# New execution order and new PSUM places for a four-layer kernel on one Trainium2 core

## The chip, the core and the metric

The kernel runs on one core of a Trainium2 chip. A core has TensorE (PE: matrix products into PSUM, eight banks), VectorE (DVE), ScalarE (ACT), GpSimd (POOL) and SyncE (SP), each with an instruction queue of its own that it executes in order, and 16 DMA engines. Engines wait for one another through semaphores. The metric is the device time of one execution in microseconds (us); times of a version are given as the median of several runs.

## What is computed

Four layers on x of 4 x 512 x 256, each `x + attention(norm(x)) + feed_forward(norm(x))`:

```
xn = layernorm(x)
L0: 16-head causal attention with alibi  + ternary-weight gated FFN (groups of 64, hidden 1024)
L1: gated recurrence: causal conv of 4, l2-normed q and k, scan mem = gamma*mem + gate*k*v, group norms
    + mixture of 16 experts, top 2, capacity 128, and a shared expert
L2: single-head attention                + gated FFN whose weights are cubic splines of control points
L3: 16-head attention with rope          + 8 experts, top 2 of a softmax, bf16, and a shared expert
    (its FFN also adds its own input xn)
```

Attention per head, as everywhere: `softmax(q k^T / sqrt(d) [+ alibi, causal]) v`, then an output projection.

## The kernel before

The kernel is written as parts. A part is a few instructions of one engine for one tile: `score` is two 64-row products of keys and queries of a group of four heads into a pair of PSUM banks (L749), from which DVE's `top` takes the maximum (L1152); `prob` is the same product with the maximum subtracted (L760), which ACT's `exp` turns into `probs` (L1670); `weigh` multiplies with the values (L770). `unit` is one of eight hidden blocks of a feed-forward layer for one batch, twelve matmuls in layer 2 (three products of high and low halves), and POOL's `low` makes the low half of its result. `tern_cast` (ACT), `tern_sum` (PE), `tern_scaled` (DVE, L1045 to L1055) and `tern_out` (POOL) make one of twelve ternary weight blocks each. `stat` (DVE), `root` (POOL, L1983) and `norm` (ACT, L1574) make the normalized rows, `turn` (PE, L710) transposes them, `turned` (ACT) and `cut_low` (DVE, L1096) split them into a high and a low half.

Keys carry the layer, the batch and tile numbers: score(0,0,0,0,3) is layer 0, batch 0, head group 0. q and k of a batch are stored to DRAM (`keep`, SP) and read back regrouped by heads (`bring`, POOL, L1965, two issues of 512 KB); the maxima take the same way (`max_keep`, `max_bring`, L1971). In layer 1 POOL's `gather` fetches each token's two expert rows from the outbox by indirect DMA, four issues for a part (L2082), after the last experts' stores. In layer 2 the spline weights are made by DVE, ACT's `spline_high` (L1875) and POOL's `spline_low` (L2090); `score2` is a row block of its attention, `top2` (DVE, L1486) and `exp2` (ACT, L1899) its softmax. In layer 3 `q_low` (DVE, L1128) is the low half of the turned q and k, and POOL's `based` (L1991) and `with_xn` (L1996) add the bias and xn to x; `mixed` (DVE, L1540) and `mix_comb` (POOL, L2100) belong to the experts.

All work around the change is ordered by hand-written numbers. `PARTS` lists the parts of each engine (1098 on PE, 844 on DVE, 857 on ACT, 429 on POOL, 165 on SP). `DUE` gives each part a turn on its engine, and `Turns` sorts by it; that order is the order of the instructions. `TAKEN` gives each part of PE its first PSUM bank: 0, 2 or 4 for those that take a pair or one of a pair, 6 or 7 for single ones. `Plan` walks PE's order, notes who held a place last, and `freed` makes the new holder wait for those that read it. All waits are counted from the order by semaphores, so a new table changes the counts that are waited for and nothing else.

## Time and profile before

| | |
|---|---|
| median of 3 runs | 1232.33 us (1230.72 to 1233.26) |
| span of the profiled execution | 1229.5 us; the page gives no time outside it |
| PE busy | 1096.5 us, 89% of the span |
| DVE / ACT / POOL busy | 864.2 / 631.2 / 503.0 us |
| mean granted TensorE clock | 0.951 of full speed |
| DMA | 116.42 MB, mean 95 GB/s |

The span runs from the first to the last instruction. An engine's busy time counts its compute instructions; the rest is idle time, and the profile names what ended it. In a row of the timeline, what stands in brackets is the idle time before the instruction and the instruction or transfer that ended it. The granted clock is TensorE's, as a share of full speed: 1.00 is 2.4 GHz, 0.5 is 1.2 GHz. A matmul that stands behind a wait in the order waits too, even if its own inputs are ready. Layers take the stretches 0 to about 360 us, to 600, to 850 and to the end, with overlaps of neighbours.

### The profile page before, as it was taken

The numbers are of one execution on the slowest core, as the hardware profiler recorded it, in microseconds if no ns is written. First come the engines' busy times: TensorE is split into PE (matmuls) and PEld (weight loads), VectorE is DVE, ScalarE is ACT, GpSimd is POOL, SyncE is SP. The second block draws the span as 40 slices with busy tenths as digits, with TensorE's granted clock in tenths as the row PEclk, the third lists the DMA queues.
The fourth block names the chain that finished last, engine by engine and source line by source line (L and its number), as shares of the span: only waits on it lengthen the run. The fifth ranks groups of instructions, "written<-read, shape, count | busy, mean of one in ns | idle before, by whom it ended". The sixth has DMA issues, their size and how long they took to land.

```text
span 1229.5 us, 17428 instructions
## 1 busy us (share of the span) xinstructions
PE 1096.5 (89%) x6541; PEld 718.4 (58%) x6556; DVE 864.2 (70%) x1612; ACT 631.2 (51%) x963; POOL 503.0 (41%) x551
## 2 busy tenths in 40 slices
PE   4579999999999998999389999998789998996998
PEld 2356686765665564675268898987234543553445
DVE  6988767678658999856667326368776779668751
ACT  4445656475568875643235224252176276455473
POOL 5655748466514544413764214053331321141131
PEclk9769999999999999999689999999699999998999
DMA  5905335443260000267350000008626316317220
GB/s 178 291 10 156 81 96 161 126 123 107 49 207 35 35 35 9 82 206 243 94 52 26 1 1 1 1 26 201 156 51 155 108 45 165 92 49 173 71 72 18
DMA packets 86115, 116.42 MB, mean 95 GB/s; under 512 B 29616, under 2 KB 43280, under 8 KB 85264
## 3 DMA queue, kind: packets, MB, share of 16 engines
q1 hardware_dynamic: 47792, 70.28, 19.1%
q0 software_dynamic: 38240, 45.03, 14.7%
q8 instruction: 52, 0.85, 0.3%
q14 instruction: 31, 0.25, 0.1%
HBM read 81.54 MB, written 40.40 MB: 99 GB/s over the span
## 4 chain that ended last, share of the span: by engine, by line
PE 64%; DVE 21%; ACT 5%; issue 4%; POOL 3%; DMA 2%; another core or an unknown queue 0%; SPq 0%; ACTq 0%; DVEq 0%; POOLq 0%
PE pair L691 22%; PE bank L691 19%; PE bank L770 7%; PE pair L760 5%; PE pair L749 5%; DVE max L1152 4%; ACT probs L1670 2%; POOL gathered L2082 1%; PE pair L710 1%; PE bank L778 1%; DVE hidden L1208 1%; DVE hidden L1206 1%; DVE tern_mask L1049 1%; PE pair L790 1%; DVE mix_h L1540 1%
## 5 line engine op out<-in xcount | busy, mean ns | idle before, releaser
L1152 DVE TENSOR_REDUCE max<-pair 128x2 f32<-128x1024 f32 (+3 forms) x256 | 252.6, 1020 | 64.1 <-PE pair L749 36.6
L1670 ACT ACTIVATE probs<-pair 128x1024 f32<-128x1024 f32 (+3 forms) x256 | 213.4, 865 | 112.9 <-PE pair L760 106.4
L749 PE MATMUL pair<-ks,qs 64*128 64x512 f32 (+3 forms) x512 | 111.7, 457 | 28.7 <-DVE max L1152 13.9
L770 PE MATMUL bank<-probs,v 128*32 128x512 f32 (+3 forms) x1024 | 119.0, 542 | 2.0 <-ACT probs L1670 1.3
L760 PE MATMUL pair<-qs,ks 64*128 64x512 f32 (+3 forms) x512 | 103.8, 437 | 13.7 <-DVE max L1152 4.9
L2003 POOL TENSOR_TENSOR h_low<-hidden,h_high 128x512 fp32r<-128x512 f32 x64 | 83.3, 1307 | 77.4 <-ACT h_high L1708 77.0
L749 PEld LDWEIGHTS pair<-ks,qs 64*128 64x128 f32 x512 | 50.8, 198 | 89.2 <-DVE max L1152 35.1
L760 PEld LDWEIGHTS pair<-qs,ks 64*128 64x128 f32 x512 | 46.5, 190 | 81.2 <-ACT probs L1670 25.9
L2100 POOL TENSOR_TENSOR h<-mix_h,h 128x512 bf16<-128x512 f32 x48 | 54.8, 1169 | 75.4 <-DMA h<-comb 49.7
L1702 ACT ACTIVATE hidden<-pair 128x512 f32<-128x512 f32 x64 | 38.0, 597 | 86.5 <-PE pair L691 72.6
L2047 POOL TENSOR_SCALAR_AFFINE_SELECT probs<-probs 128x256 f32<-128x256 f32 x128 | 51.3, 411 | 65.0 <-ACT probs L1670 63.8
L1189 DVE TENSOR_TENSOR x<-bank,x 128x512 f32<-128x512 f32 x32 | 21.9, 686 | 78.6 <-PE bank L691 78.6
L1206 DVE SCALAR_TENSOR_TENSOR hidden<-hidden,pair 128x512 f32<-128x512 f32 x64 | 43.8, 684 | 41.6 <-ACT hidden L1702 41.4
L1965 POOL DMA_DIRECT2D qs<-kept x32 | 24.2, 755 | 119.4 <-DMA kept<-q_low 52.7
L1708 ACT CAST h_high<-hidden 128x512 fp32r<-128x512 f32 x64 | 39.1, 620 | 48.7 <-DVE hidden L1208 29.7
L1971 POOL DMA_DIRECT2D qs<-kept_max x32 | 24.8, 776 | 88.2 <-DMA kept_max<-max_rows 87.3
L691 PE MATMUL pair<-x,w_in 128*128 128x512 bf16 x179 | 47.4, 400 | 5.5 <-DVE mix_h L1540 1.4
L1926 ACT ACTIVATE mix_t<-pair 128x512 f32<-128x512 f32 x48 | 28.5, 599 | 44.1 <-PE pair L691 42.5
L691 PE MATMUL bank<-wo,rowsT 128*128 128x256 f32 x192 | 48.8, 385 | 1.1 <-ACT rowsT L1691 1.1
L1540 DVE SCALAR_TENSOR_TENSOR mix_h<-mix_t,pair 128x512 f32<-128x512 f32 x48 | 32.7, 685 | 22.8 <-ACT mix_t L1926 16.4
L691 PE MATMUL pair<-cut_high,w_in 128*128 128x512 f32 x128 | 45.1, 436 | 2.9 <-POOL w_in L1977 2.2
L1574 ACT ACTIVATE xn<-x,shift,rstd 128x256 f32<-128x256 f32 x64 | 36.0, 599 | 19.9 <-POOL shift L1985 19.9
(327 smaller groups left out, 2678.5 us busy)
## 6 DMA issues: line engine op xcount, KB each, us to landing
kept<-q_high SPq DMA_DIRECT2D x64, 256.0 KB, 3.7
qs<-kept POOLq DMA_DIRECT2D x32, 512.0 KB, 4.2
ks<-kept POOLq DMA_DIRECT2D x32, 512.0 KB, 5.2
kept<-q_low SPq DMA_DIRECT2D x32, 256.0 KB, 4.1
expert_in<-in_experts_in SPq DMA_DIRECT2D x16, 352.0 KB, 4.3
expert_out<-in_experts_out SPq DMA_DIRECT2D x16, 256.0 KB, 5.5
h<-comb SPq DMA_DIRECT2D x4, 1024.0 KB, 5.4
x<-in_x SPq DMA_DIRECT2D x4, 512.0 KB, 5.1
```

The lines of the kernel that those rows point to most:

```text
L691: made = mm(out, lhsT, rhs, start=start and n == 0, stop=stop and n == len(pairs) - 1)
L749: made = mm(to[:, hh, 0:n], m.qs[k][slot][r0:r0 + STACK, p, qt * P:(qt + 1) * P], m.ks[k][slot][r0:r0 + STACK, p, 0:n], start=True, stop=k ...
L760: made = mm(to[:, hh, q0:T], m.ks[k][slot][r0:r0 + STACK, p, kt * P:(kt + 1) * P], m.qs[k][slot][r0:r0 + STACK, p, q0:T], start=True, stop ...
L770: made = mm(to[32 * j:32 * j + 32, q0:T], m.v[b % 2][:, kt, G * g + j, :], m.probs[(2 * kt + j // 2) % 4][:, j % 2, q0:T], start=kt == 0, ...
L1152: V.tensor_reduce(m.max[:, g % 2, :, p, qt], to[:, :, 0:n], AX.X, ALU.max).then_inc(*s.done("top"))
L1206: V.scalar_tensor_tensor(h[:, :], h[:, :], 1.0, to[:, 0, :], ALU.add, ALU.mult).then_inc(*dve.up())
L1540: V.scalar_tensor_tensor(h, m.mix_t[j % 2][:, :], 1.0, to[:, 1, :], ALU.add, ALU.mult).then_inc(*s.done("mixed"))
L1670: A.activation(m.probs[(2 * kt + p) % 4][:, :, q0:T], to[:, :, q0:T], ACT.Exp, scale=0.25).then_inc(*s.done("exp"))
L1708: A.copy(m.h_high[k][:, j, :], m.hidden[k][j % 2][:, :]).then_inc(*s.done("high"))
L2003: Q.tensor_tensor(m.h_low[k][:, j, :], m.hidden[k][j % 2][:, :], m.h_high[k][:, j, :].bitcast(F32), ALU.subtract).then_inc(*s.done("low"))
L2047: Q.affine_select(corner, corner, [[0, 2], [1, P]], ALU.is_ge, 0.0, base=0, channel_multiplier=-1).then_inc(*s.done("causal"))
L2100: Q.tensor_tensor(m.h16[:, j, :], m.mix_h[j % 2][:, :], m.h16[:, j, :], ALU.mult).then_inc(*s.done("mix_comb"))
```

## The change

Only numbers of `DUE` and `TAKEN` are replaced: the turns of parts on all five engines, and the PSUM places. They were chosen on the mean of several drawn sets of durations and landings. The parts, their instructions, their tiles in SBUF and the transfers stay the same, and so do all functions.

661 of PE's 1098 parts keep their position, 435 of DVE's 844, 365 of ACT's 857, 138 of POOL's 429 and 94 of SP's 165. Most others move by a few positions; by five or more move 7 parts on PE, 27 on DVE, 44 on ACT, 24 on POOL and 3 on SP. 259 parts of PE get another first bank, among them 53 of score, 55 of prob, 40 of weigh and 20 of unit.

The core of the diff: the rows of which the tables differ most, and those of the parts named above. Numbers are in the order of the keys.

```diff
 DUE = {...
-    "tern_sum": "0 2 3 4 7 9 8 10 17 15 16 26",
-    "turn": "1 52 144 207 375 432 444 469 582 598 623 646 664 711 829 952",
+    "tern_sum": "0 1 3 4 7 10 8 9 16 14 17 27",
+    "turn": "2 52 143 207 375 432 445 468 582 598 623 645 654 711 829 952",
...
-    "root": "2 20 47 63 101 171 239 258 288 291 297 309 315 320 337 348",
-    "based": "6 48 52 78 319 330 342 364",
-    "with_xn": "322 332 344 366",
+    "root": "2 19 46 66 102 171 245 258 288 292 299 305 315 324 336 345",
+    "based": "6 49 53 82 319 330 347 412",
+    "with_xn": "326 346 378 413",
...
-    "gather": "283 285 286 287 289 290 293 292",
-    "spline_low": "276 277 280 279 278 281 282 284 296 294 295 298",
+    "gather": "284 285 286 287 289 291 293 294",
+    "spline_low": "276 277 278 281 282 279 280 283 295 290 297 296",
...
 TAKEN = {...
-    "tern_sum": "040400240442",
-    "turn": "2224040202422044",
+    "tern_sum": "200400240442",
+    "turn": "2244004202042044",
...
-    "qk2": "4420",
-    "v2": "76766767",
-    "score2": "6776676766677676",
-    "probs_turn": "7676677667767776",
+    "qk2": "0200",
+    "v2": "76766776",
+    "score2": "6777677677667766",
+    "probs_turn": "7676677667766776",
```

The moves that the prediction speaks of, read out of the tables: on PE tern_sum(1) goes ahead of turn(0,0), score(0,0,0,0,3) ahead of unit(0,0,5), and unit(2,0,3) ahead of score2(0,3). The place of score2(0,3) in PSUM is then freed by exp2(0,1) and no longer by exp2(0,0). On DVE gated(2,0,0), combine(2,3), weight2(0,2) and combine(2,2) go ahead of top2(0,0), with top2(0,1) right behind it, and two maxima, top(3,0,3,1,2) and top(3,0,3,1,1), ahead of q_low(3,1,0). On ACT tern_cast(2) goes among the first norms and tern_cast(3) ahead of turned(0,0). On POOL bring(0,0,0) goes behind bring(0,0,1), tern_out(5), two low, a sum and bring(0,0,2); spline_low(2,1) ahead of gather(0,0); with_xn(1) and based(3,2) from 800 and 828 us to behind root(3,3); with_xn(2) from 843 us to ahead of mix_comb(1,8); based(3,3) and with_xn(3) behind bring(3,3,3).

## Rows read from the trace of the kernel before

**Rows 1.** The page: span, busy times by engine, the chain that ended last.
```profile
span 1229.5 us, 17428 instructions
PE 1096.5 (89%) x6541; PEld 718.4 (58%) x6556; DVE 864.2 (70%) x1612; ACT 631.2 (51%) x963; POOL 503.0 (41%) x551
...
PE 64%; DVE 21%; ACT 5%; issue 4%; POOL 3%; DMA 2%; another core or an unknown queue 0%; SPq 0%; ACTq 0%; DVEq 0%; POOLq 0%
```

**Rows 2.** Stretches: length, busy of PE, PEld, DVE, ACT, POOL, clock, DMA, GB/s.
```profile
0.00:30.00 30.00, 11.92 (x37) 7.49 (x37) 20.21 (x38) 13.69 (x23) 17.11 (x20) 1.00 0.58 181
30.00:90.00 60.00, 39.04 (x199) 27.05 (x203) 52.63 (x92) 27.05 (x46) 37.07 (x37) 0.74 0.51 155
90.00:360.00 270.00, 262.93 (x2266) 180.60 (x2265) 189.94 (x357) 161.31 (x260) 154.73 (x230) 1.00 0.42 126
360.00:570.00 210.00, 195.96 (x802) 122.41 (x801) 174.90 (x398) 137.85 (x217) 81.47 (x64) 0.98 0.25 80
570.00:630.00 60.00, 37.06 (x142) 24.62 (x140) 35.14 (x77) 17.23 (x33) 41.10 (x43) 0.80 0.55 117
660.00:840.00 180.00, 179.44 (x1036) 158.98 (x1035) 89.43 (x168) 65.61 (x119) 56.26 (x43) 1.00 0.05 13
930.00:1140.00 210.00, 187.17 (x1068) 94.31 (x1073) 157.69 (x269) 110.22 (x136) 48.99 (x53) 0.95 0.43 110
```

**Rows 3.** PE's waits: what was waited for, us in total, times, longest.
```profile
PE pair L710 <- ACT xn L1574: 20.4, 2, 18.6
PE pair L749 <- DVE max L1152: 13.9, 23, 1.3
```

**Rows 4.** DVE's timeline at 15 us: start, us, line, operation.
```profile
14.97 0.69 DVE L1045 TENSOR_SCALAR tern_scale<-pair 128x512 bf16<-128x512 f32 x1 [1.43 <-PE pair L702]
```

**Rows 5.** PE's timeline, first projection and first score.
```profile
21.13 0.80 PE L691 MATMUL pair<-cut_high,wqk_high 128*128 128x512 f32 x1 [0.53 <-DVE cut_low L1096]
...
63.65 0.50 PE L749 MATMUL pair<-ks,qs 64*128 64x512 f32 x2 [2.96 <-DVE tern_mask L1055]
```

**Rows 6.** Three more stretches, columns as in the second group.
```profile
624.10:627.00 2.90, 2.90 (x14) 2.37 (x13) 1.36 (x4) 2.32 (x4) 2.29 (x3) 1.00 0.85 73
633.00:639.00 6.00, 6.00 (x17) 4.70 (x16) 5.76 (x15) 1.03 (x2) 0.00 (x0) 0.54 0.40 36
922.00:926.00 4.00, 4.00 (x20) 1.51 (x12) 2.75 (x4) 1.70 (x3) 0.00 (x0) 0.60 0.98 229
```

**Rows 7.** L1965 from 30 to 70 us: issues, and their time to landing.
```profile
L1965 POOL DMA_DIRECT2D qs<-kept x3: 716/762/798, 41.0 to 49.4; - x3
...
DMA to landing us min/median/max: 7.7/9.7/13.1
```

**Rows 8.** L2082, 584 to 606 us: ns min/median/max, first, last start.
```profile
L2082 POOL DMA_INDIRECT gathered<-outbox,slots x16: 945/949/1179, 584.6 to 604.7; - x16
```

**Rows 9.** POOL's timeline among these gathers.
```profile
589.46 1.28 POOL L2090 TENSOR_TENSOR w_in_low<-spline_raw,w_in_high 128x512 fp32r<-128x512 f32 x1
```

**Rows 10.** ACT's timeline ahead of them.
```profile
585.41 0.62 ACT L1875 CAST w_in_high<-spline_raw 128x512 fp32r<-128x512 f32 x1 [3.36 <-DVE spline_raw L1460]
```

**Rows 11.** PE's timeline at 632 us.
```profile
632.34 1.22 PE L691 MATMUL bank<-cut_high,qk 128*128 128x512 f32 x2 [4.00 <-ACT probs L1899]
```

**Rows 12.** DVE's timeline from 630 us.
```profile
630.59 0.69 DVE L1486 TENSOR_REDUCE top<-bank 128x1 f32<-128x512 f32 x1 [4.21 <-remote]
...
631.39 1.80 DVE L1435 SCALAR_TENSOR_TENSOR x<-gathered,weights,x 128x256 f32<-128x256 f32 x2
```

**Rows 13.** L1128, whole span: ns min/median/max, first and last start.
```profile
L1128 DVE TENSOR_TENSOR q_low<-turned_raw,q_high x8: 1217/1224/3746, 834.0 to 1112.5; 128x1024 fp32r<-128x1024 f32 x8
```

**Rows 14.** POOL's timeline, with_xn(3) and the idle time before a max_bring.
```profile
915.29 2.44 POOL L1996 TENSOR_TENSOR x<-x,xn 128x1024 f32<-128x1024 f32 x1
...
1160.13 0.76 POOL L1971 DMA_DIRECT2D qs<-kept_max  x1 [4.94 <-DMA kept_max<-max_rows]
```

**Rows 15.** PE's timeline at 920 us.
```profile
920.01 0.50 PE L749 MATMUL pair<-ks,qs 64*128 64x512 f32 x2 [0.81 <-DVE max L1152]
```

More of the change, by code:

```diff
@@ L325 @@
-    "prob": "2220042002044000204242442202024020242024424204420002200424202224242420240242202040222400020224240442044042040202242024040240424022424402244220422200220204240242042022420040244044044440024404404204224004402020002422420204024024022004240442404424024442000420",
-    "weigh": "77776666666666666666666677776666666677777777777766666666666666667777666666666666777766667777666677776666777777777777777777776666",
-    "back": "77677667666677777776767676766677",
-    "rows": "402004020442",
-    "out": "76677767666776767676766776667667",
@@ L330 @@
-    "unit": "2402020420004202220202044042044220422040024204202044200424402044",
-    "down": "77767677",
-    "mean": "6777",
-    "proj": "0044022402200440",
-    "gate": "7766667776676776",
+    "vals": "2020224404004244",
+    "score": "4404002400444040204022042420022420044404024240044042004400404442402044024224200020040044024400020040204204400020204020220044424002020424022244442440440240420040022442200424040402024404020002222004042204424244042024044424000242242404444202222240204200440220",
@@ new lines @@
+    "prob": "4202242002042400424044222202024020242024024204420022200442404224242420240242202040222402020224240442040442040202224202400422404022424402244224422200220202420442002022420040044044044440024404000202442000402022002422020204040404022004240402404422044442000420",
+    "weigh": "66666666666677776666666677776666777766667777777766666666666666666666777766666666666677776666777777776666777777777777777777776666",
+    "back": "67677677766677767776676776776676",
+    "rows": "442004040244",
+    "out": "67767767766776767666776777667676",
@@ L335 @@
+    "unit": "2402020420004202220242044002244240422040424024024422040442404404",
+    "down": "77666677",
+    "mean": "7776",
+    "proj": "0444022002200440",
+    "gate": "7666666767666776",
     "gamma": "4024",
     "inflow_turn": "0202",
-    "mem_turn": "77777677",
-    "shared": "0202440220420402",
-    "count": "6666",
+    "mem_turn": "77777666",
+    "shared": "0202440240420422",
+    "count": "7766",
     "logit_turn": "7777",
     "merge": "76",
-    "expert_turn": "6676777777676666",
@@ L343 @@
[L343 to L352 removed]
+    "expert_turn": "6677777777676666",
+    "expert_in": "4204242042400204",
+    "expert_fold": "7767666667767667",
+    "expert_out": "6667766676766767",
@@ L353 @@
+    "spline": "424024202404",
+    "qk2": "0200",
+    "v2": "76766776",
+    "score2": "6777677677667766",
+    "probs_turn": "7676677767766776",
+    "comb_turn": "7766",
+    "mix": "402042020240040402024220200402424220242402004224",
 }.items()}
```

8 lines of the change are left out of this document (removed), and 262 rows, old and new, of the table DUE.

## The prediction, made before the changed kernel had run

> **What bounds the kernel now.** I read the page first. [rows 1] gives a span of 1229.5 us with PE busy in 1096.5 of them (89%), and a chain that lies 64% on PE and 21% on DVE. So 133 us of idle time on PE is all that an order can win, plus what TensorE's clock gives back. Then I cut the span into stretches [rows 2]. From 90 to 360 us PE is busy 262.9 of 270, from 660 to 840 us 179.4 of 180. No order makes those much shorter, but a badly placed part can make them longer. The idle time stands elsewhere: 18.1 us before 30; 21.0 from 30 to 90, with DVE at 52.6 of 60 and the granted clock at 0.74; 14.0 from 360 to 570; 22.9 from 570 to 630, clock 0.80; 22.8 from 930 to 1140. Last I read PE's list of waits [rows 3]: the largest single one is 18.6 us for the normalized rows of layer 2 (xn, L1574), and 13.9 us in 23 pieces are for the row maxima (L1152), 0.6 us each.
>
> The whole change is order. Since each engine executes in order, its parts do the same work; a move costs or gains only where the moved part is at the head of its engine while another engine waits for what lies behind it. I compared the two tables part by part and looked up in the trace where every part that moves stands. Most moves swap neighbours: on PE seven parts of 1098 move five places or more. I cost the five places where a move meets a wait that the trace shows, and bound the rest.
>
> **Place 1, the start.** PE now does tern_sum(1) before turn(0,0). Before, it stood behind turn(0,0), and DVE waited 1.43 us for it, until 14.97 [rows 4]. DVE's ternary block can start 1.43 us earlier, and with it cut_low(0,0), which follows the block and which the first projection at 21.13 waits for [rows 5]. Against it: turn(0,0) now takes the place in PSUM that tern_scaled(0) reads, and two ternary casts go ahead of ACT's turned(0,0). Both lie beside DVE's block, so they cost nothing unless they take longer than the 4.7 us left of it (21.13 - 14.97 - 1.43). The first projection gains 1.4 us, and DVE, busy 52.6 of the next 60 us, carries that forward. At 63.65 PE has waited 2.96 us for its chain, at score(0,0,0,0,3) [rows 5]. unit(0,0,5), which had been done ahead of that wait, now stands behind it, and its matmuls, 2.9 us for a unit's twelve [rows 6] or less, lose their cover. But DVE bounds this stretch, and nothing is added to it. I take the 1.4 as kept, between 2.4 gained (one more collision of POOL with DVE gone) and 1.5 lost (2.9 - 1.4).
>
> The other edit here: on POOL bring(0,0,0), issued at 41.0, goes behind bring(0,0,1), bring(0,0,2) (49.4) and work between, so to about 51. Such an issue took 7.7 to 13.1 us to land here, median 9.7 [rows 7]. It lands at 60.7 by the median, 64.9 by the slowest with its second half 0.8 later; its first reader runs at 63.65, after a wait for DVE. I take nothing, and keep 1.3 us lost (64.9 less 63.65) as a bound.
>
> **Place 2, the gathers before layer 2.** The 18.6 us wait is a chain through POOL: sixteen gathers, 0.95 us each, first start 584.6, last 604.7 [rows 8], and behind them root(2,0), whose result the norms and then turn(2,0) wait for. In the new table spline_low(2,1), which stood inside that row at 589.46 with 1.28 us [rows 9], comes before the first gather. It needs ACT's spline_high, which starts at 585.41 and takes 0.62 [rows 10]. So: ready at 586.03, done at 587.3, first gather 587.3 - 584.6 = 2.7 us late; and the 1.28 us inside the row go. The row ends 2.7 - 1.3 = 1.4 us late, and root(2,0) with it. This is a loss at full price, since PE does nothing else there. Bounds: 0, if spline_high comes as much earlier, and 2.7.
>
> **Place 3, the hole at 632.** PE stood 4.00 us for the probabilities (L1899) [rows 11], because DVE started the maximum of score2(0,0) at 630.59 after 4.21 us which the trace puts on nothing in the kernel ("remote") [rows 12]. Two edits meet here. PE puts unit(2,0,3) before score2(0,3); a unit's matmuls, 624.1 to 627.0, take 2.9 us [rows 6], so 2.9 of the 4.0 are filled with work that had to be done anyway. But score2(0,3) also gets another place, which the second next exponential, exp2(0,1), frees instead of exp2(0,0). And DVE puts gated(2,0,0), combine(2,3), weight2(0,2) and combine(2,2) ahead of that maximum, top2(0,1) right behind it. combine(2,3) took 1.80 us in the old order [rows 12], combine(2,2) 1.0, gated 1.4, weight2 0.65 and top2 0.85, in the same timeline: 5.7 in all. If the stall stays after the same number of DVE's instructions, score2(0,3) can start 5.7 us later than at 632.34, and 5.7 - 2.9 = 2.8 are lost. If there is no stall, it is 4.2 less: 1.4 gained. The row shows the stall once and not what makes it. I take half of it (2.1), which gives 0.7 lost, and keep both ends. Behind the hole the clock was 0.54 for 6 us [rows 6], 6 x (1 - 0.54) = 2.8 us; that it comes back is a bound for the good case alone.
>
> **Place 4, POOL beside DVE at 915.** q_low of the rope layer (L1128) takes 1.22 us by the median of eight, and 3.75 once [rows 13]: at 915, where POOL runs with_xn(3) (L1996, 2.44 us) [rows 14]. 1.22 + 2.44 = 3.66, so DVE stood still for the length of POOL's operation. PE then waits 0.81 us for one maximum [rows 15] and 0.6, the mean of such waits [rows 3], for the next, and from 922 to 926 its clock is 0.60 [rows 6], which costs 4 x 0.4 = 1.6. The change puts based(3,3) and with_xn(3) behind bring(3,3,3), into POOL's 4.94 us of idle time before 1160.13 [rows 14]. They would take 2 x 2.44 = 4.9, just what is free. DVE also takes two maxima (top(3,0,3,1,2) and its neighbour) ahead of q_low now, the ones that PE waits for. Gain: 1.4 at least, 1.4 + 1.6 = 3.0 at most; I take 2.6, for DVE is late by 2.5 us for everything behind q_low. The Trainium skill (SBUF — State Buffer, "Who interferes with whom") says that a DVE operation with both inputs in SBUF and a GpSimd operation that reads SBUF hold one shared port pair in turn, each for a whole instruction, and that a maximum (tensor_reduce) never takes part. The trace agrees with its first half (3.75 us beside 1.22); by that rule the new places beside maxima cost nothing, and DVE gets back 2.44 us, so the sum would be 0.2 us worse than with my 2.6.
>
> **Place 5, everything else.** Some 150 parts of score, prob and weigh get other PSUM places or swap, and ACT and DVE swap their partners. Where PE is 97 to 100% busy, they have no idle time to win. In 360 to 570 and 930 to 1140 there are 14.0 and 22.8 us of idle time [rows 2], in gaps under 3 us each. I take 0; a tenth of these 37 us either way is 4 us.
>
> Sum: -1.4 + 1.4 + 0.7 - 2.6 + 0 = -1.9 us on the profiled span: 1229.5 to 1227.6. The median of the runs stands 2.8 us above that span, so 1232.3 - 1.9 = 1230.4, 0.15% faster. About 0.2% (2.5 us) is what a measurement of this kernel can tell from no change.
>
> **Rivals.** (A) The good ends come together: DVE's stall is gone (-1.4 for place 3), with it the low clock behind it (-2.8), the start gives 2.4 and place 4 gives 3.0. -2.4 + 1.4 - 1.4 - 2.8 - 3.0 = -8.2, so 1224.1. For it: the clock was low right behind both holes [rows 6], and nothing in the kernel makes the stall. Against: with no stall at all there is still a wait for exp2(0,1).
>
> (B) The stall stays whole: it goes to gated(2,0,0), the instruction that now stands there, and the five parts behind it. Place 3 costs 2.8, the start gives nothing under unit(0,0,5): 0 + 1.4 + 2.8 - 2.6 = +1.6, so 1233.9. For it: in the old order the four moved parts took just the DVE time behind the stall.
>
> (C) Slower, by one mechanism: a score or prob part's new place in PSUM is still being read for its last owner when PE comes to it, in order, so that PE stands and its clock falls. The pair at 920 is the measure: 0.8 us and 1.6 by the clock, 2.4 each. Against -1.9 for the rest, one new one gives +0.5, two +2.9 (1235.2), three +5.3 (1237.6), four +7.7; it decides from two on. For it: 53 score and 55 prob places change, and 23 waits for a maximum stand already [rows 3]. Against: nearly all swaps are with the next neighbour, and PE finds work at once in 97% of 90 to 360.
>
> **How the numbers follow.** My forecast 0.36, (A) 0.22, (B) 0.20, (C) 0.22. The forecast's own range is 1227 to 1234, one bound of one term either way. The range over all cases reaches from 1221 (A with a tenth of the idle time of place 5 won) to 1240 (C with four holes). Faster by over 0.2% (below 1229.9): 0.17 of the forecast, (A), and 0.02 of (B) and (C) by place 5: 0.41. Within 0.2%: 0.17 of the forecast, 0.08 of (B), 0.02 of (C): 0.27. Slower (above 1234.8): the rest, 0.32.
>
> **What would show it.** Place 1: the first L691 near 19.7 instead of 21.13. Place 2: the first gather 2.7 us later against ACT's spline_high and turn(2,0)'s wait 1.4 us longer. Place 3: the gap before score2(0,3), 4.00 us before, between 2.6 (no stall) and 6.8 (whole stall), and which DVE instruction stands behind "remote". Place 4: L1128 with a longest time near 1.25 us, and no gap of 0.81 us behind it. Place 5: PE's busy time in 90 to 360 and 660 to 840 as before. I am wrong if new gaps over 1 us stand in the attention stretches behind DVE's maxima with a clock of 0.6, or if PE's busy time grows where it was full.

## The result and the profile after

The new order is slower: 1240.11 us by the median of four runs (1236.77 to 1241.41), against 1232.34 for the kernel before in the same comparison. The ratio is 1.0065 [1.0048, 1.0083], so 7.8 us more. The prediction said 1230.4 us. The profiled execution has a span of 1237.9 us, 8.4 above that of before. Medians here and below leave out executions over 1.5% above the fastest of their kernel, which was one execution in all.

The page, as [rows 1] for the kernel before:

```profile
span 1237.9 us, 17417 instructions
...
PE 1108.4 (90%) x6542; PEld 724.8 (59%) x6556; DVE 844.2 (68%) x1612; ACT 630.4 (51%) x964; POOL 500.4 (40%) x551
...
PE 62%; DVE 17%; ACT 8%; issue 4%; DMA 4%; POOL 3%; SPq 1%; ACTq 0%; DVEq 0%; POOLq 0%
```

PE's idle time did not grow. It was 1229.5 - 1096.5 = 133.0 us and is 1237.9 - 1108.4 = 129.5. PE's busy time grew, by 11.9 us for the same matmuls. The mean granted clock fell from 0.951 to 0.945. Over the spans, 1229.5 x 0.049 = 60 us of full speed were missing before and 1237.9 x 0.055 = 68 are missing now, about as much more as the spans differ. Nobody who looks for new waits alone finds that, and the prediction looked for waits. In PE's list of waits, the two largest of [rows 3] are shorter, and one that was 2.0 us has become 7.2:

```profile
PE pair L710 <- ACT xn L1574: 18.8, 2, 16.0
PE pair L749 <- DVE max L1152: 12.1, 22, 1.5
...
PE pair L702 <- DVE hidden L1208: 7.2, 1, 7.2
```

The last one stands in layer 0, at 55 us, and comes up again under place 1.

To find the place, I took how much later each of PE's parts starts than the same part in the kernel before, and cut both spans where this lag changes. Stretches of the two kernels then hold the same matmuls. The kernel before, layer 1, the experts with the splines, and the head of layer 2 (length, then busy time and instructions of PE, PEld, DVE, ACT and POOL, granted clock, DMA share, GB/s):

```profile
360.00:541.00 181.00, 167.76 (x682) 103.86 (x681) 159.50 (x368) 129.37 (x196) 77.16 (x60) 0.97 0.16 53
541.00:611.00 70.00, 50.33 (x208) 31.74 (x207) 42.19 (x87) 19.05 (x45) 30.24 (x29) 0.88 0.60 182
611.00:660.00 49.00, 41.22 (x180) 33.21 (x178) 36.58 (x73) 20.48 (x36) 28.92 (x28) 0.86 0.45 55
```

The same three, and below them layer 3, in the kernel after:

```profile
360.00:547.50 187.50, 169.91 (x682) 104.83 (x681) 156.11 (x353) 131.67 (x198) 77.84 (x60) 0.97 0.16 51
547.50:633.00 85.50, 66.61 (x208) 39.81 (x208) 40.46 (x83) 18.56 (x44) 29.69 (x29) 0.74 0.47 146
633.00:675.00 42.00, 38.67 (x180) 31.51 (x179) 35.39 (x75) 18.86 (x34) 28.32 (x28) 0.91 0.45 71
...
854.90:1237.90 383.00, 340.05 (x1944) 174.17 (x1955) 264.93 (x436) 194.02 (x240) 104.26 (x106) 0.95 0.42 107
```

Layer 1 takes 6.5 us more, 4.4 of them idle time. The experts and splines take 15.5 more: 208 matmuls need 66.6 us instead of 50.3, while the idle time stays (19.7 and 18.9). The mean clock there fell from 0.88 to 0.74; 70 x 0.12 = 8.4 us of full speed were missing before, 85.5 x 0.26 = 22.2 are missing now, so the clock explains at most 13.8 of the 16.3 us of busy time. The head of layer 2 gives back 7.0, and layer 3 (840 to 1229.5 before, 389.5 us) gives back 6.5. The sum is 6.5 + 15.5 - 7.0 - 6.5 = 8.5; layer 0 and the rest of layer 2 are nearly even in this execution.

PE's timeline where the experts' stretch turns bad, before:

```profile
558.12 1.15 PE L960 MATMUL pair<-cubics,powers 16*128 16x512 f32 x6
559.08 1.04 PE L961 MATMUL pair<-cubics,powers 32*128 32x512 f32 x6
560.06 1.13 PE L691 MATMUL bank<-expert_out,expert_hT 128*128 128x256 f32 x4
```

and after:

```profile
564.67 1.12 PE L960 MATMUL pair<-cubics,powers 16*128 16x512 f32 x2
565.64 1.02 PE L961 MATMUL pair<-cubics,powers 32*128 32x512 f32 x2
566.58 1.13 PE L691 MATMUL bank<-expert_out,expert_hT 128*128 128x256 f32 x4
...
573.38 2.07 PE L960 MATMUL pair<-cubics,powers 16*128 16x512 f32 x2
575.25 1.91 PE L961 MATMUL pair<-cubics,powers 32*128 32x512 f32 x2
...
577.57 1.91 PE L691 MATMUL bank<-expert_out,expert_hT 128*128 128x256 f32 x4
...
603.02 1.22 PE L960 MATMUL pair<-cubics,powers 16*128 16x512 f32 x1 [2.38 <-DVE cubics L1443]
```

`spline(c, n)` multiplies rows 32n to 32n + 32 of its inputs, so the three parts n = 0, 1, 2 of one c use different rows of TensorE. In the old order they stood side by side, and the next product starts 560.06 - 558.12 = 1.9 us after the first of the three (x6 records in the time of x2). In the new order expert_out(11) stands behind the first, which takes 566.58 - 564.67 = 1.9 us alone. From 573 on even one part takes 3.7 us (573.38 to 577.09), since the clock has gone to its lower level. The windows around it, in the kernel after:

```profile
564.00:568.60 4.60, 4.60 (x16) 2.25 (x15) 2.48 (x6) 0.53 (x3) 0.00 (x0) 1.00 1.02 326
568.60:589.10 20.50, 20.50 (x40) 10.04 (x39) 9.56 (x14) 3.58 (x10) 3.75 (x3) 0.50 0.43 139
```

PE had no idle time by its records from 564 to 589, and still the granted clock stood at 0.50, 1.2 GHz, for 20.5 us. Its last wait before the fall was 0.24 us, at 548.6; from then on it had done experts' and output products and the first single splines. In the kernel before no interval at the lower level stands between 488.3 and 594.1 us.

What followed hung on this. Up to 560 us the new order is 6.6 us late; its last expert's product ends at 598.7 instead of 581.6, 17.1 us late. So 10.5 us were lost between, and 20.5 us at half speed are 10.3 us of full speed. Behind that product, PE's merge and last splines come late as well (splines at 611.8 to 615.6, before they were done at 588.9), and DVE waits for them with the gathered rows' sums queued behind:

```profile
615.51 0.69 DVE L1457 TENSOR_TENSOR spline_step<-pair,spline_mask 128x512 f32<-128x512 f32 x1 [6.90 <-PE pair L961]
```

### The profile page after: what moved, and what is told of

Read it like the earlier page. It is cut to its first block, busy times and chain, and to the rows that moved or that the text cites. A ratio compares the mean times of both kernels' runs of the same rounds, so it can differ in the third digit from the quotient of the medians.

```text
span 1237.9 us, 17417 instructions
## 1 busy us (share of the span) xinstructions
PE 1108.4 (90%) x6542; PEld 724.8 (59%) x6556; DVE 844.2 (68%) x1612; ACT 630.4 (51%) x964; POOL 500.4 (40%) x551
## 3 DMA queue, kind: packets, MB, share of 16 engines
q1 hardware_dynamic: 47792, 70.28, 18.9%
## 4 chain that ended last, share of the span: by engine, by line
PE 62%; DVE 17%; ACT 8%; issue 4%; DMA 4%; POOL 3%; SPq 1%; ACTq 0%; DVEq 0%; POOLq 0%
PE pair L691 22%; PE bank L691 17%; PE bank L770 7%; DVE max L1152 5%; PE pair L760 4%; PE pair L749 4%; DMA ks<-kept 2%; ACT probs L1670 2%; SPq L2114 1%; PE pair L960 1%; DVE x L1435 1%; PE bank L778 1%; PE pair L710 1%; PE pair L961 1%; DMA x<-in_x 1%
## 5 line engine op out<-in xcount | busy, mean ns | idle before, releaser
L749 PE MATMUL pair<-ks,qs 64*128 64x512 f32 (+3 forms) x512 | 109.9, 451 | 26.9 <-DVE max L1152 12.1
L1965 POOL DMA_DIRECT2D qs<-kept x32 | 24.0, 750 | 138.2 <-DMA kept<-q_low 64.4
L1189 DVE TENSOR_TENSOR x<-bank,x 128x512 f32<-128x512 f32 x32 | 21.8, 688 | 78.9 <-PE bank L691 78.9
L1708 ACT CAST h_high<-hidden 128x512 fp32r<-128x512 f32 x64 | 39.2, 616 | 36.4 <-PE bank L691 18.9
L691 PE MATMUL bank<-wo,rowsT 128*128 128x256 f32 x192 | 49.9, 390 | 2.1 <-ACT rowsT L1691 1.1
L691 PE MATMUL pair<-x,w_in 128*128 128x512 bf16 x180 | 46.7, 399 | 5.0 <-ACT probs L1670 1.4
L691 PE MATMUL pair<-cut_high,w_in 128*128 128x512 f32 x128 | 46.1, 444 | 5.5 <-DVE tern_mask L1055 3.6
L1208 DVE TENSOR_TENSOR hidden<-pair,hidden 128x512 f32<-128x512 f32 x64 | 44.3, 691 | 2.2
```

The source lines that it names most:

```text
L691: made = mm(out, lhsT, rhs, start=start and n == 0, stop=stop and n == len(pairs) - 1)
L749: made = mm(to[:, hh, 0:n], m.qs[k][slot][r0:r0 + STACK, p, qt * P:(qt + 1) * P], m.ks[k][slot][r0:r0 + STACK, p, 0:n], start=True, stop=k ...
L1208: V.tensor_tensor(h[:, :], to[:, 1, :], h[:, :], ALU.mult).then_inc(*s.done("gated"))
L1708: A.copy(m.h_high[k][:, j, :], m.hidden[k][j % 2][:, :]).then_inc(*s.done("high"))
```

## The experiments

Each kernel takes the tables of one version and puts a stretch of turns and places of the other in. Ratios are against the kernel before, run on the same chip (its medians there: 1231.7, 1231.5, 1232.0 and 1231.4 us in the four groups). The medians of the kernel before differ by up to 1.0 us between groups (1232.34 in the first comparison), and so much may stand in a difference between kernels of two groups; two kernels of these groups whose intervals overlap are not told apart with certainty. Profiles are of one execution each, and not always of a typical one: with the experts as before, with layer 1 new and with layer 0 new it was the fastest of all. So the verdicts go by medians. "Lag" is how much later PE's parts start than in the profile of before.

**After, with the experts and splines as before.** The turns of PE's parts 535 to 581 and of their neighbours on all engines go back (90 turns, 13 places). Part of it:

```diff
-    "spline": "549 551 552 553 555 559 566 575 580 576 581 579",
+    "spline": "549 550 551 555 554 559 566 575 576 578 579 580",
-    "cubic": "411 414 423 432",
+    "cubic": "411 413 421 428",
...
-    "merge_low": "438 445",
+    "merge_low": "434 440",
```

> The changed kernel with the orders and PSUM places of one stretch put back to those of before: the last experts of layer 1 and the spline weights (PE parts 535 to 581, and the blocks of DVE, ACT, POOL and SP beside them). Theory 1: this stretch alone makes the change slow. Against before, PE's parts are 6.5 us late before it and 22.1 us late at the start of layer 2, so 15.6 us are lost here; undone, the kernel comes to 1240.1 - 15.6 = 1224.5. Rival 2: part of that is slack that the next stretch gives back in any case (7.2 us of the 22.1 were won back by 660 us); then only 8.4 are gained, 1231.7. Rival 3: the low clock from 568.6 to 589.1 is set by what comes ahead of this stretch; then it stays and the time is near 1240.

1229.28 us, ratio 0.9985 [0.9961, 1.0009]: 10.8 us below the kernel after by the medians, 9.9 by the two ratios (1.0065 - 0.9985 of 1232). The same work takes 71.0 us, against 85.5 and 70.0:

```profile
547.00:618.00 71.00, 51.42 (x207) 32.61 (x206) 41.56 (x87) 18.88 (x44) 29.97 (x29) 0.86 0.56 176
```

That is between theory 1 and rival 2, nearer to rival 2. The intervals of this kernel and of the kernel after are apart, so the loss in the stretch is shown. What follows it (-7 in the head of layer 2, -6 in layer 3) does not depend on it.

**After, with only PE's splines as before.** PE's turns 549 to 581 alone (11 turns, 8 places):

```diff
-    "merge": "577 578",
+    "merge": "577 581",
...
-    "spline": "549 551 552 553 555 559 566 575 580 576 581 579",
+    "spline": "549 550 551 555 554 559 566 575 576 578 579 580",
```

> The changed kernel with only PE's order and places of parts 549 to 581 put back: spline(0,0), (0,1), (0,2) side by side again, and (2,1) with (2,2), (3,0) with (3,1). DVE, ACT, POOL and SP keep the changed order. Theory 1a: a spline's products use rows 0 to 15 or 0 to 31 of a third of PE each, side by side they run at the same time (three in 2.0 us in the trace of before), apart they take 2.0 each, and with them apart the clock falls at 568.6 for 20.5 us; undone, about 10 us come back: 1230. Rival: it is the order of DVE and ACT; then 2 us or less, 1238 to 1240.

1233.83 us (nine executions), 1.001 [0.9978, 1.0041]: 6.3 of the 10.8 us by the medians, 6.8 of 9.9 by the ratios. In the profile the stretch takes 78.9 us, 60.71 of them busy, and the clock is at its lower level from 570.9 to 584.5. With the rest of the stretch new, PE's order is worth more than half of the loss; the next kernels show that this share holds in this company alone.

**After, with the gathers first.** The move of place 2 goes back, and with it gather(2,1) and gather(3,*) ahead of spline_low(3,0) and one turn of root (6 turns, all of POOL).

```diff
-    "gather": "284 285 286 287 289 291 293 294",
+    "gather": "283 285 286 287 289 290 293 292",
-    "spline_low": "276 277 278 281 282 279 280 283 295 290 297 296",
+    "spline_low": "276 277 278 281 282 279 280 284 295 294 297 296",
```

> The changed kernel with only POOL's order put back at two places: gather(0,0) ahead of spline_low(2,1), and gather(2,1), gather(3,*) ahead of spline_low(3,0). Theory 2: the first gather starts 5.9 us after the end of the last expert's product instead of 3.0 us, so 2.9 us come back: 1237.2. Rival: root(2,0) waited for DVE's stat in the changed kernel (3.25 us), so an earlier gather gives less: 0 to 1 us, 1239 to 1240.

1242.76 us, 1.0083 [1.0056, 1.011], nothing gained. The gathers go ahead of spline_low again, but root(2,0), which they were to release, had waited 3.25 us for DVE in the kernel after, and now waits 4.69. First the kernel after, then this one:

```profile
627.85 1.22 POOL L1983 TENSOR_TENSOR rstd<-rstd,minus_half 128x4 f32<-128x4 f32 x1 [3.25 <-DVE rstd L1083]
```

```profile
629.67 1.22 POOL L1983 TENSOR_TENSOR rstd<-rstd,minus_half 128x4 f32<-128x4 f32 x1 [4.69 <-DVE rstd L1083]
```

DVE's sums of the gathered rows stand behind the spline work that waited 6.9 us for PE. In this kernel POOL does not bound the way to layer 2, and the price of place 2 falls away.

**Before, with layer 3 new.** All moves of the last layer alone (432 turns), those of place 4 among them.

```diff
-    "based": "6 48 52 78 319 330 342 364",
+    "based": "6 48 52 78 319 330 347 412",
-    "with_xn": "322 332 344 366",
+    "with_xn": "322 346 378 413",
```

> The kernel of before with the changed orders and places from about 850 us on alone (layer 3). Theory 3: the changed order wins there, for PE's parts are 14.4 us late at 850 and 7.3 us late at 960: 6.8 us by the end, so 1232.3 - 6.8 = 1225.5. Rival: what is won back there was only lateness (loads and stores that did not wait once everything was late); then no change, 1231 to 1233.

1226.17 us, 0.9953 [0.9927, 0.9979]: 5.5 us won. No q_low takes over 1228 ns.

**Before, with the splines apart.** The reverse of the second kernel, for the first cubics only:

```diff
-    "expert_out": "511 509 517 512 531 523 534 530 547 546 557 552 571 568 574 573",
+    "expert_out": "511 509 517 512 531 523 534 530 547 546 557 550 571 568 574 573",
...
-    "spline": "549 550 551 555 554 559 566 575 576 578 579 580",
+    "spline": "549 551 552 553 555 559 566 575 576 578 579 580",
```

> The kernel of before with one edit: PE takes expert_out(11) between spline(0,0) and spline(0,1), and spline(1,0) and fold(10) ahead of spline(1,1), as the changed order does, with its PSUM places for parts 549 to 574. Theory 1a: three splines that stand side by side take 2.0 us together, apart 2.0 for the first and 1.9 or more for the others; and the clock falls behind them for up to 20.5 us as in the changed kernel. Then 2 us by the overlap and up to 10 by the clock are lost: 1234 to 1243. Rival 4: the clock falls only because the whole stretch comes later and DVE and ACT stand in another order; then no more than 2 us, 1231 to 1234.

1232.73 us, 1.0007 [0.9982, 1.0031]: no difference that can be measured. Its profiled execution, the slowest of its ten (1238.4), does show what the overlap was worth. From the first spline to the part behind the three and expert_out(11), 561.03 - 558.12 = 2.9 us passed in the kernel before, and 563.22 - 557.45 = 5.8 pass here, at full clock:

```profile
557.45 1.12 PE L960 MATMUL pair<-cubics,powers 16*128 16x512 f32 x2
...
563.22 0.44 PE L948 MATMUL bank<-ident_r,expert_h 128*128 128x128 f32 x2
```

Behind it the clock is at half from 565.0 to 578.7, and the lag grows by 7.6 us in all. Nine executions were faster, and their mean clocks were 0.944 to 0.954 against 0.945 here. So a long fall can come with this order, but probably does not come in most of its executions; the order of PE's products by itself doesn't decide it.

**Before, with the rest of that stretch new.** The first splines stay side by side, everything else of the stretch is new (84 turns).

```diff
-    "cubic": "411 413 421 428",
+    "cubic": "411 414 423 432",
...
-    "merge_low": "434 440",
+    "merge_low": "438 445",
```

> The complement: the kernel of before with all that the change moves in the stretch of the last experts and splines (DVE, ACT, POOL, SP, and PE behind part 575), but the first three splines side by side on PE as before. Theory 1a: without the fall of the clock near 570 only the rest is lost, PE idle and the gathers' delay, 5 us: 1237. Rival 4: the order of DVE and ACT makes the loss: 1242 to 1247.

1238.76 us, 1.0062 [1.0044, 1.008]: 7.3 us lost, nearly the whole of the 10.8. The clock is at half from 563.3 to 577.0 and from 590.6 to 600.9.

**After, with layer 1 as before** (265 turns, 24 places):

```diff
-    "gamma": "438 456 464 491",
+    "gamma": "438 453 466 491",
-    "count": "431 448 465 486",
+    "count": "431 452 464 487",
```

> The changed kernel with the orders and places of layer 1 put back, 360 to 546 us of before (PE parts 427 to 534 and the blocks beside them). PE's parts were 0.3 us late ahead of this stretch and 6.5 behind it. Theory: 6.2 us come back, 1233.9. Rival: the stretch behind it (experts) starts by the arrival of weights or by the inbox, not by PE; then less than 2 us, 1238 to 1240.

1237.49 us, 1.0069 [1.0038, 1.0101]: 2.6 us less than the kernel after by the median, nothing by the ratio (1.0065 there). Inconclusive for the time. In the profile layer 1 costs 1.6 us now (the lag is 2.4 at 360 and 4.0 at 541) instead of 6.5, and the next stretch costs as much as in the kernel after.

**Before, with layers 2 and 3 new.** What both earlier groups point to: old layers 0 and 1 and old experts, new from the head of layer 2 on.

> The kernel of before with the changed orders and places from the start of layer 2 (611 us) to the end. Layer 3 alone gave -5.5 us. In layer 2's first 40 us the changed kernel won back 7.2 us against the profile of before, of which 3.1 were also won by the kernel with layer 3 alone changed, whose layer 2 is that of before. Theory: the filled hole (unit(2,0,3) ahead of score2(0,3)) is worth 7.2 - 3.1 = 4.1: 1226.2 - 4.1 = 1222. Rival: DVE's stall whole, +2.8: 1229.

1220.18 us (1217.59 to 1224.06), 0.9918 [0.9888, 0.9948]. It is 11.3 us faster than the kernel before, and so beats both kernels. Its span is 1218.4 us, and its experts' stretch, head of layer 2 and layer 3:

```profile
541.30:613.00 71.70, 54.30 (x209) 33.91 (x207) 41.40 (x87) 19.10 (x45) 30.06 (x29) 0.82 0.57 174
613.00:655.20 42.20, 39.01 (x183) 32.20 (x182) 33.60 (x71) 18.88 (x34) 28.21 (x27) 0.91 0.45 70
...
834.20:1218.40 384.20, 343.84 (x1959) 174.81 (x1957) 266.00 (x436) 193.76 (x240) 104.32 (x106) 0.94 0.42 107
```

49.0 to 42.2 and 389.5 to 384.2: 6.8 and 5.3 us, the same two gains as in the kernel after.

**Before, with POOL's moves of layer 3 alone** (77 turns, all of POOL; with_xn and based as above).

> The kernel of before with one engine's order changed in layer 3, POOL's: with_xn(1) and based(3,2) behind root(3,3), with_xn(2) ahead of mix_comb(1,8), based(3,3) and with_xn(3) behind bring(3,3,3), and the swaps of low and mix_comb between. All else is that of before. Theory (place 4 of the prediction): q_low takes 1.22 us everywhere instead of 3.75 once, and 1.4 to 3.0 us are gained: 1228.5 to 1230. Rival: the gain of layer 3 (5.5 us) comes from the orders of the maxima on DVE and scores on PE; then POOL alone gives under 0.5 us.

1234.2 us, 1.0024 [0.9993, 1.0054]. The eight q_low take 1215 to 1226 ns, and from 840 to 945 us the lag falls from +0.4 to -5.4, 5.8 us won. Then it is given back: -2.1 at 975, -3.4 at 990, 0.0 at 1170. POOL now has max_bring(3,1,0) ahead of mix_comb(1,1), and stands for a transfer; DVE and PE stand behind it (what takes the rest, behind 1040 us, was not read):

```profile
969.44 0.76 POOL L1971 DMA_DIRECT2D qs<-kept_max  x1 [18.95 <-DMA kept_max<-max_rows]
...
971.48 0.69 DVE L1540 SCALAR_TENSOR_TENSOR mix_h<-mix_t,pair 128x512 f32<-128x512 f32 x1 [1.98 <-POOL h L2100]
...
972.23 0.50 PE L749 MATMUL pair<-ks,qs 64*128 64x512 f32 x2 [1.48 <-DVE mix_h L1540]
```

The mechanism of place 4 is right, and alone it is worth nothing that can be measured; with the other engines' turns of layer 3 the layer wins 5.5.

**Before, with the hole at 632 filled alone** (57 turns, 3 places; the moves of place 3 and their neighbours).

```diff
-    "score2": "586 588 585 589 608 618 605 606 635 629 632 630 656 654 652 657",
+    "score2": "587 588 585 590 608 618 605 606 635 629 632 630 656 654 652 657",
...
-    "top2": "462 473 460 475 497 512 492 494 533 524 527 529 556 555 553 558",
+    "top2": "465 466 460 475 497 512 492 494 533 524 527 529 556 555 553 558",
```

> The kernel of before with only the hole at 632 us changed: PE parts 583 to 597 (unit(2,0,3) ahead of score2(0,3), which gets the place that exp2(0,1) frees), DVE's 461 to 479 (gated(2,0,0), two combines and weight2(0,2) ahead of top2(0,0)) and ACT's 493 to 525 in the changed order. Layers 2 and 3 together gave 6.0 us more than layer 3 alone. Theory: it is this hole, 4 to 6 us, 1226 to 1228. Rival (B of the prediction): DVE's stall stays whole and 2.8 us are lost; the 6 us come from elsewhere in layer 2.

1238.53 us, 1.0059 [1.0037, 1.0082]: 6.6 us lost. The hole is closed, and two others open 14 and 34 us later:

```profile
633.01 0.73 PE L691 MATMUL bank<-cut_high,qk 128*128 128x512 f32 x2 [0.69 <-ACT probs L1899]
...
646.29 1.22 PE L691 MATMUL pair<-cut_high,w_in_high 128*128 128x512 f32 x2 [4.74 <-DVE hidden L1208]
...
666.19 1.19 PE L691 MATMUL pair<-cut_high,merged 128*128 128x512 f32 x2 [4.46 <-DVE cut_low L1096]
```

**Old cubics, and old ACT, in the kernel with the rest new.** Two kernels, each one piece of the 7.3 us put back: DVE's turns of cubic and spline_sum with their neighbours (9 turns), and ACT's of the experts and spline_high (17 turns).

```diff
-    "cubic": "411 414 423 432",
+    "cubic": "411 413 421 428",
-    "spline_sum": "413 415 416 419 418 420 427 431 434 433 436 435",
+    "spline_sum": "414 415 416 419 418 420 427 432 434 433 436 435",
```

```diff
-    "spline_high": "459 463 461 470 471 475 474 480 483 481 492 484",
+    "spline_high": "459 461 462 467 464 470 476 480 483 481 492 484",
```

> The kernel with the first splines side by side and the rest of the experts' stretch new (it was 7.3 us slower than before), but DVE's cubic(1), cubic(2) and cubic(3) where they were before, ahead of the last experts' work. Theory 5: PE waited 2.4 us for cubic(3) with spline(3,0) and the clock fell behind it (602.8 to 609.6 in the changed kernel); undone, 2.4 + 3.4 = 5.8 of the 7.3 come back: 1233. Rival 6: it is ACT's order of spline_high; then nothing changes, 1239.

> The same kernel (first splines side by side, rest of the experts' stretch new), but ACT's order of parts 453 to 476 as before: each spline_high right behind its spline_sum instead of behind the experts' copies and activations. Theory 5: the cubics are the cause and nothing changes here, 1239. Rival 6: 4 us or more come back, 1235 or less.

The first: 1233.91 us, 1.0027 [0.9999, 1.0055]; 4.9 of the 7.3 us come back. The second: 1240.74 us, 1.0068 [1.0037, 1.01]; nothing does. ACT's turns don't count. The cubics do, as far as these two intervals can tell ([1.0044, 1.008] before, which overlaps that of the first a little).

**Before, with the cubics late alone.** The same nine turns, put into the kernel before: cubic(1), cubic(2) and cubic(3) one to four turns later on DVE.

```diff
-    "cubic": "411 413 421 428",
+    "cubic": "411 414 423 432",
```

> The kernel of before with one edit on DVE: cubic(1) behind spline_sum(0,0), cubic(2) behind expert_gated(12), cubic(3) behind spline_sum(2,1). With the experts' stretch new, taking these back gave 4.9 us. Theory 5: cubic(3) late makes PE wait with spline(3,0), and what follows comes late by that and by the clock; alone 3 to 6 us: 1235 to 1238. Rival: only together with the new order of spline(2,2) and merge, behind which PE has nothing; then 0 to 2 us, 1232 to 1234.

1233.81 us, 1.0033 [1.0015, 1.0052]: 2.5 us, and its executions spread from 1231.0 to 1240.6. In the profiled one PE waits for the cubic, the clock is at half from 560.9 to 574.6, and this stretch takes 77.3 us with 60.0 busy (70.0 and 50.3 before):

```profile
559.03 1.09 PE L960 MATMUL pair<-cubics,powers 16*128 16x512 f32 x2 [1.17 <-DVE cubics L1443]
...
537.40:614.70 77.30, 59.99 (x209) 35.78 (x207) 41.56 (x87) 19.07 (x46) 30.10 (x30) 0.76 0.53 165
```

**Before, with layer 1 new, and with layer 0 new.** The mirror of the seventh kernel, and the one stretch that nothing had tested.

```diff
-    "tern_sum": "0 2 3 4 7 9 8 10 17 15 16 26",
+    "tern_sum": "0 1 3 4 7 10 8 9 16 14 17 27",
-    "turn": "1 52 144 207 375 432 444 469 582 598 623 646 664 711 829 952",
+    "turn": "2 52 143 207 375 432 444 469 582 598 623 646 664 711 829 952",
```

> The kernel of before with layer 1 alone new (360 to 546 us, PE parts 427 to 534). In the profile the changed kernel lost 6.2 us there, and with that put back it was faster by 2.6 us at the median. Theory: 3 to 6 us slower, 1235 to 1238. Rival: the loss in one profile was chance, or the loads of the expert weights absorb it; 1231 to 1234.

> The kernel of before with layer 0 alone new (0 to 360 us). Place 1 of the prediction: 1.4 us gained, between 2.4 and -1.5, and 1.3 lost if bring(0,0,0) lands late. In the profiles of the changed order PE's parts are 3.1 us late at 45 us and 0.0 to 3.4 us late at 300, in those of the old order 0.0 to 2.9. Theory: nothing within 1 us, 1231 to 1233. Rival: the 3.1 us at 45 us stay, 1235.

Layer 1 new: 1243.71 us (1235.34 to 1249.82), 1.0117 [1.0086, 1.0149]. Layer 0 new: 1240.95 us (1231.59 to 1249.33), 1.0095 [1.0065, 1.0126]. Both ratios are above that of the whole change. In the profile of layer 1 new the lag goes from -2.8 us at 345 to +5.4 at 540, and all of these 8.2 us are idle time: 21.3 us against 13.2 in the same stretch of the kernel before. Rows of its PE timeline that the kernel before lacks and the kernel after has, with waits within 0.1 us of these:

```profile
416.60 1.14 PE L929 MATMUL bank<-ident_r,logit_rows 32*128 32x32 f32 x8 [2.31 <-DVE slots L1410]
...
438.75 3.70 PE L691 MATMUL pair<-conv,wgamma 128*128 128x512 f32 x8 [1.32 <-DVE gates L1260]
...
470.41 1.98 PE L691 MATMUL bank<-conv,wgates 128*128 128x512 f32 x4 [1.80 <-ACT gates L1748]
...
513.00 0.44 PE L936 MATMUL bank<-ident_r,tokens 128*128 128x128 f32 x2 [1.60 <-DVE x L1189]
```

In the profile of layer 0 new PE is 3.8 us late at 45, 5.5 at 60 and 2.9 from 285 us on.

But these two profiles are of the fastest execution of six each, 1235.34 and 1231.59 us, 8.4 and 9.4 below the medians. So they hold a third of the loss of layer 1 and none of that of layer 0. What is on record of the other five is the mean clock: 0.955 in both profiled executions, 0.943 to 0.952 in the others with layer 1 new and 0.938 to 0.945 with layer 0 new. Over all six it is 0.945 with layer 0 new against 0.951 for the kernel before beside it, 0.006 x 1240 = 7.4 us of full speed, most of the 9.6. For layer 1 new it is 0.948, 3.7 of the 12.4. Where and why the clock was lower in them, no trace shows.

**Layers 2 and 3 new, with the hole as before.** The best version, less the 57 turns of place 3.

```diff
-    "score2": "587 588 585 590 609 618 607 606 633 630 629 634 658 653 652 656",
+    "score2": "586 588 585 589 609 618 607 606 633 630 629 634 658 653 652 656",
```

> The kernel with layers 2 and 3 new (1220.2), but with the hole at 632 us as before: PE parts 583 to 597, DVE's 461 to 479, ACT's 493 to 525. Filling the hole alone, in the kernel of before, lost 6.6 us. Theory 7: the gain of layer 2 (6.0 us) comes from the hole together with the gathers and root(2,1) that follow it; with the hole as before it is gone: 1226. Rival 8: the hole's edit is a loss anywhere and the gain comes from POOL's order; then this kernel is faster still, 1214 to 1220.

1223.33 us, 0.9948 [0.993, 0.9967], so 3.1 us slower than with the new turns; the two intervals overlap a little. The same edit costs 6.6 us alone and wins some 3 in company: in the version with layers 2 and 3 new none of the gaps at 646 and 666 exists, presumably for the later turns that go with it.

Differences of medians, in us. First column: new instead of old, against the kernel before. Second: old instead of new, against the kernel after.

```
stretch                 in before      in after (put back)
layer 0                   + 9.6         not tried
layer 1                   +12.4         - 2.6 (none by the ratio)
experts and splines       + 7.3 (*)     -10.8
layers 2 and 3            -11.3         not tried
all                       + 7.8
(*) with the first splines left side by side
```

The single figures add to about +18, the whole is +7.8. A stretch of one order joined to a stretch of the other brings waits of its own, so a figure of this table is that of a piece with its seams.

## Why the prediction was wrong

**The failed step is place 5, "everything else. I take 0; a tenth of these 37 us either way is 4 us".** The loss lies there, in two parts. Putting the experts' and splines' stretch back gave 10.8 us, and layer 1 new cost 12.4 us alone (putting it back in the kernel after gave 2.6 at most; the profile of the kernel after shows 6.5). Two arguments behind the 0 were wrong. One was that a swap of neighbours moves little. In the profile of layer 1 new, such moves add 8.1 us of idle time on PE; four of its waits, 1.3 to 2.3 us each, stand in the rows above. That each comes from a part which another engine waits for and which went behind its neighbour is argued, for no single swap was undone. The other was that only idle time can be lost, so that idle time bounds the price. Of the 15.5 us of the experts' stretch none is idle time. Up to 13.8 of it is the lower clock. Part of the rest is that products which ran side by side no longer do: that took 2.9 us in the profile with the splines apart. What brings the lower clock was found only in part: late cubics lengthen it, and why is open. [rows 2] had the clock at 0.80 from 570 to 630, and the sum had a clock term for the good case of place 3 alone, none for a loss. The signs of being wrong that the prediction named did not come. PE is busy 263.2 us from 90 to 360 and 178.8 from 660 to 840, as before; its busy time grew where it had not been full.

**Place 1 (-1.4) didn't come.** The first L691 starts at 20.73 instead of 21.13, 0.4 us earlier, not 1.4:

```profile
20.73 0.79 PE L691 MATMUL pair<-cut_high,wqk_high 128*128 128x512 f32 x1
...
65.31 0.50 PE L749 MATMUL pair<-ks,qs 64*128 64x512 f32 x2 [1.49 <-DVE tern_mask L1055]
```

score(0,0,0,0,3) comes at 65.31 instead of 63.65. The step that was missed is on SP. There the load of extra0 (kept<-in_extra_q and in_extra_k), issued at 42.12 before, goes ahead of the load of x1, which is issued at 39.35 instead of 37.48. DVE's statistics of that x wait for it (they had no wait before). Behind them stand a ternary block and the products of `unit` (hidden, L1208), for which PE stands 7.19 us until 55.58. In the profile of layer 0 new the two waits are 4.43 and 8.79 us. The kernel after:

```profile
39.35 0.58 SPq L2114 DMA_DIRECT2D x<-in_x  x1
...
48.93 0.43 DVE L1074 BATCH_NORM_STATS2 stats<-x 128x6 f32<-128x256 f32 x1 [2.83 <-DMA x<-in_x]
...
55.58 1.03 PE L702 MATMUL pair<-tern_mag,groups 128*128 128x512 bf16 x2 [7.19 <-DVE hidden L1208]
```

In the kernel before, PE's waits there were 4.38 and 2.04 us. Much of this lateness is gone again by 120 us, where PE is 1.4 us late. The other edit here, bring(0,0,0), was issued at 54.3 and not at 51, and its reader at 65.31 waited for DVE, so it cost nothing, as forecast. Layer 0 new on its own costs 9.6 us by the median, for which no term stood. Which of its 626 turns costs it stays open.

**Place 2 (+1.4): the mechanism is seen, the price isn't paid.** In the kernel after, spline_low runs at 603.18, behind ACT's spline_high, and the first gather right behind it; it starts 5.9 us after the last expert's product instead of 3.0:

```profile
603.18 1.26 POOL L2090 TENSOR_TENSOR w_in_low<-spline_raw,w_in_high 128x512 fp32r<-128x512 f32 x1 [2.50 <-ACT w_in_high L1875]
604.59 1.03 POOL L2082 DMA_INDIRECT gathered<-outbox,slots  x1 [0.15 <-issue]
```

Undoing it won nothing, since the statistics behind the gathers were what root(2,0) waited for. turn(2,0) waits 16.0 us and not the 20.0 of the prediction, because PE itself comes to it later.

**Place 3 (+0.7, between -1.4 and +2.8) took a stall that comes and goes for one that stays.** DVE's stall of 4.21 us "remote" is absent from the kernel after and from three others read for it (experts as before, layer 3 new, layers 2 and 3 new). It is not a thing of one execution, though. With late cubics alone it is there again, at the first top2:

```profile
630.43 0.69 DVE L1486 TENSOR_REDUCE top<-bank 128x1 f32<-128x512 f32 x1 [4.09 <-remote]
```

It is 2.13 us with layer 1 new, 1.64 with the hole filled alone and 1.45 in the kernel with the cubics put back; in the remaining profiles it is at most 0.6. In the kernel after, the five parts had no stall to be moved past, and the gap of 4.00 us before score2(0,3) is gone. The head of layer 2 gained 7.0 us, more than the good end of 1.4 + 2.8, of which the 57 turns of place 3 are worth some 3 when the later turns go with them.

**Place 4 (-2.6) was right in its mechanism.** q_low takes at most 1.22 us (3.75 before, [rows 13]):

```profile
L1128 DVE TENSOR_TENSOR q_low<-turned_raw,q_high x8: 1215/1221/1225, 850.8 to 1120.0; 128x1024 fp32r<-128x1024 f32 x8
```

A second DVE operation went the same way, the scaling of the shared weights. It took 2671 ns before, where it started at 842.95 beside another with_xn (842.94, 2.39 us), and takes 418 after; the prediction had overlooked it:

```profile
L1059 DVE TENSOR_SCALAR shared_w<-shared_w x1: 418/418/418, 858.3 to 858.3; 128x512 f32<-128x512 f32 x1
```

The Trainium skill (SBUF — State Buffer, "Who interferes with whom") says that a DVE operation with two inputs in SBUF, as q_low is, and a GpSimd one that reads SBUF hold one shared port pair in turn; the 3.75 us beside 1.22 agree with it. What the step left out was POOL's own queue: its moves alone win 5.8 us and give them back, 2 to 3 of them behind a max_bring that stands ahead of a mix_comb. Layer 3 as a whole gained 5.5 to 6.5, twice the term.

**Of the rivals none was it.** (C) had the right sign and its three or four holes gave 1237.6 to 1240.0, but its mechanism, new places in PSUM that PE must wait for, isn't what the waits of the kernel after show: 12.1 us for maxima instead of 13.9. The range ended at 1240 and the time is 1240.1.

**What stays open.** Why the clock falls near 566 us, and why it stays low for so long, isn't settled. In the one profiled execution of each kernel, the interval at the lower level that starts between 560 and 575 us is 20.5 us long in three kernels with the late cubics (after, after with the gathers first, after with layer 1 as before), and 10.2 to 13.7 in the four others that have them. In the eleven with the cubics as before it is 3.4 or missing, but for 13.7 with the splines apart. So a fall comes in 15 of the 18, with the old cubics too; what goes with the late cubics is its length. But the late cubics alone cost 2.5 us by the median, not 7 to 10, so they make a long interval likelier, and what makes it sure wasn't found. Nor was it tried how the +12.4 and +9.6 of layers 1 and 0 split among their turns, or what of them is the seam.

## What to carry to other kernels

When an order changes, ask of each stretch not only what waits, but what its busy time is made of: products that ran side by side, and a clock that is already below full in a stretch, can be lost with no new wait on the page. Compare stretches that hold the same instructions in both kernels; the sum over the span hides a stretch of +15 behind others of -7. An order that wins as a whole or loses as a whole is best cut by stages and tried in pieces: here the second half of the slower order behind the first half of the old one is 0.8% faster than the kernel before, where the whole is 0.65% slower.

## What the runs showed of the hardware

- Products of 16 and 32 rows on different rows of TensorE overlap when they are issued one behind another: three splines took 1.9 us together, and the first took 1.9 us alone. The Trainium skill says so too (TensorE: Matmul & The Clock Gate, "The mechanism" of packing small matmuls): products on different row groups of the array overlap. The trace agrees. What the case adds is that one large product put between them ends the overlap of the first with the rest (2.9 us became 5.8).
- The granted clock stood at 0.50 for 20.5 us (568.6 to 589.1) behind a stretch in which PE's records leave no idle time from 548.6 us on. Here a low clock did not follow a wait.
- Kernels with the same layer 0 stand apart already there: the lags at 120 us of those that have the old one run from -2.8 to +3.5. Single times of one kernel spread by 4 to 18 us. Medians of six to twelve runs were needed for 0.3%, and a stretch of a profile has to be read from its own start.
- DVE's stall for nothing in the kernel [rows 12] was 4.21 and 4.09 us in two of 18 profiled executions, 1.45 to 2.13 in three, and at most 0.6 in the others. Such a stall is no fixed term for a sum; it wants a second execution, and then a chance.
